# A macaron block on one core: the last chunk of the second feed-forward part in split fp16, and the row sums of the attention's output at another place

## The reference

```
x = x + 0.5 * ffn(layernorm(x))
x = x + attention(layernorm(x))
x = x + 0.5 * ffn(layernorm(x))

ffn(x):  m = k0 * x[s-1] + k1 * x[s] + k2 * x[s+1]        # mixing of neighbouring rows
         h = m @ W1[p] + b1[p];  y[p] = h @ W2[p] + b2[p]     # 9 paths of width 64
         best = argmax(tanh(m @ Wo1 + bo1) @ Wo2 + bo2)
         return layernorm(x + y[best]) * gamma + beta

attention(x): q, k, v = x @ W.T + b
         weights = softmax(abs(q @ k.T / 16), causal)
         return (weights @ v) @ Wo.T + bo
```

## Time and profile before

| what | value |
|---|---|
| median of 3 runs | 1481.22 us (1480.94 to 1482.33) |
| the profiled execution | 1480.94 us |
| its span, first to last instruction | 1479.2 us |
| mean granted TensorE clock | 0.969 |
| TensorE busy | 1353.5 us (92%) |
| VectorE busy | 1168.7 us (79%) |
| ScalarE busy | 926.0 us (63%) |
| GpSimd busy | 315.9 us (21%) |

### The profile page before, as it was taken

The page is one execution under the profiler, slowest core; times in us unless marked ns, Lnnn a source line. Parts: engine busy times, 40 slices in busy tenths (PEclk is TensorE's granted clock), DMA queues, the critical chain, the costliest instruction groups (busy, mean ns, idle before and its releaser), DMA issues.

```text
span 1479.2 us, 25761 instructions
## 1 busy us (share of the span) xinstructions
PE 1353.5 (92%) x7572; PEld 786.7 (53%) x7572; DVE 1168.7 (79%) x2327; ACT 926.0 (63%) x1733; POOL 315.9 (21%) x359
## 2 busy tenths in 40 slices
PE   3999999958999999998968999999998959999995
PEld 2567776734455454544434455454544436777764
DVE  5999998766777777778867777777778857989986
ACT  5666766265666757665755666757665766776641
POOL 2255544440101000000040101000000023555422
PEclk9899999979999999999989999999999969999998
DMA  5143433210010000103010010000103021333221
GB/s 155 50 126 105 119 107 91 88 58 1 29 44 16 28 29 1 44 0 113 2 45 1 29 44 16 28 29 0 44 0 114 1 74 50 105 106 107 91 77 59
DMA packets 86995, 82.26 MB, mean 56 GB/s; under 512 B 8540, under 2 KB 86885, under 8 KB 86885
## 3 DMA queue, kind: packets, MB, share of 16 engines
q1 hardware_dynamic: 86884, 80.91, 18.1%
HBM read 55.43 MB, written 25.46 MB: 55 GB/s over the span
## 4 chain that ended last, share of the span: by engine, by line
PE 74%; DVE 8%; issue 8%; ACT 6%; POOL 2%; DMA 0%; ACTq 0%; DVEq 0%; POOLq 0%; SPq 0%
PE PS L1411 63%; PE PS L1606 3%; PE PS L1419 2%; PE PS L1507 2%; PE PS L1480 1%; DVE R L973 1%; ACT R L1261 1%; POOL R L578 1%; ACT R L1298 1%; ACT R L1302 1%; DVE st L711 1%; PE PS L1489 1%; DVE R L967 1%; DVE R L795 1%; POOL y_rstd L568 1%
## 5 line engine op out<-in xcount | busy, mean ns | idle before, releaser
L1411 PE MATMUL PS<-R 128*128 128x512 f16 (+3 forms) x3456 | 715.1, 362 | 29.3 <-DVE R L973 20.3
L1411 PEld LDWEIGHTS PS<-R 128*128 128x128 f16 (+1 forms) x3456 | 327.5, 98 | 394.1 <-DVE R L973 35.3
L973 DVE TENSOR_TENSOR R<-R 128x512 f16<-128x512 f32 (+3 forms) x288 | 188.7, 655 | 97.4 <-ACT R L1302 96.0
L1289 ACT ACTIVATE R<-PS 128x512 f32 (+5 forms) x288 | 160.2, 558 | 164.9 <-PE PS L1411 164.4
L1298 ACT ACTIVATE R<-R 128x512 f32 (+4 forms) x288 | 169.6, 589 | 51.4 <-DVE R L967 49.9
L1411 PE MATMUL PS<-R,w_hi 128*128 128x512 f16 x640 | 196.9, 390 | 4.3 <-DVE R L780 4.3
L967 DVE TENSOR_TENSOR R<-R,max_row 128x512 f32 (+4 forms) x288 | 187.2, 650 | 7.7 <-ACT max_row L1335 7.7
L1411 PE MATMUL PS<-w_hi,R 128*128 128x256 f16 x1024 | 187.7, 273 | 4.8 <-DVE R L786 4.8
L1302 ACT ACTIVATE R<-R 128x512 f16<-128x512 f32 (+3 forms) x288 | 171.1, 594 | 26.4
L545 POOL TENSOR_SCALAR veps<-mv 128x4 f32<-128x4 f32 x48 | 13.5, 280 | 801.2 <-DVE mv L718 658.1
L961 DVE TENSOR_TENSOR run_max<-run_max,R 128x512 f32<-128x512 f32 (+3 forms) x272 | 174.0, 640 | 9.3 <-DVE run_max L961 1.7
(11 more groups left out here) (116 smaller groups left out, 1710.4 us busy)
## 6 DMA issues: line engine op xcount, KB each, us to landing
R<-x_scratch SPq DMA_DIRECT2D x48, 512.0 KB, 4.5
x_scratch<-R SPq DMA_DIRECT2D x32, 512.0 KB, 3.1
R<-oh_scratch SPq DMA_DIRECT2D x32, 320.0 KB
R<-in_L_attn_x SPq DMA_DIRECT2D x16, 512.0 KB, 5.4
R<-oh_scratch SPq DMA_DIRECT2D x32, 256.0 KB
out<-R SPq DMA_DIRECT2D x16, 512.0 KB, 3.1
R<-in_L_ffn_W SPq DMA_DIRECT2D x2, 288.0 KB
R<-in_L_ffn_W SPq DMA_DIRECT2D x1, 512.0 KB
```

Source lines behind the costliest of these rows:

```text
L973: v.tensor_tensor(p_lo[:, i * TT + lo:(i + 1) * TT], pf[:, (i % 2) * TT + lo:(i % 2 + 1) * TT], p_hi[:, i * TT + lo:(i + 1) * TT], ALU.sub ...
L1289: a.activation(cols(ring, ring_m + i * TT + lo, TT - lo), ps_s[:, i, lo:], ACT.Abs, scale=1.0 / (QS * XS * D ** 0.5)).then_inc(abs_done, 1)
L1411: ins = t_.matmul(dst, w, xx, start=start and n == 0, stop=stop and n == last, skip_group_check=skip)
```

## The change

`whole` is now true in `ffn(0)` only. In `ffn(1)` chunk 4 is split like the others: ScalarE has `masked_high` for a third group, VectorE `masked_low` for a third group (behind that of the second), and TensorE three fp16 products per row group where it had one in fp32. `groups_before` counts three groups per tile there. In the attention, `output` on VectorE now calls `output_sums` itself: behind the output of row group u the sums of u - 1, and behind the last both that are left. The blocks of sums in `first_pair` are gone. At the end of a batch the order is what it was.

```
-            return c == LAST
+            return ph == 0 and c == LAST
...
-            return use(ph, t) * (len(GROUPS) - 1)
+            return t * (len(GROUPS) - 1) if ph == 0 else NTT * (len(GROUPS) - 1) + t * len(GROUPS)
...
                                            scalar=rden[:, u:u + 1], in1=cols(rows, u * D, D),
                                            op0=ALU.mult, op1=ALU.add).then_inc(x2_done, 1)
+                    if u >= 1:
+                        output_sums(s, u - 1, rows)
+                    if u == SUB - 1:
+                        output_sums(s, u, rows)
+
                 def output_sums(s, u, rows):
                     dve.wait_ge(x2_done, SUB * s + u + 1)
                     v.bn_stats(sums_at(s, u), cols(rows, u * D, D)).then_inc(x2_sums, 1)
...
                     def first_pair(i):
-                        if i == 0:
-                            for u in range(SUB):
-                                output_sums(s - 2, u, xr)
                         if is_int(j, NT - 1):
                             for u in ((), (0, 1), (2,), (3,), ())[i]:
                                 output(s - 1, u, xr_beside)
-                            if i == SUB:
-                                for u in range(SUB):
-                                    output_sums(s - 1, u, xr_beside)
...
                 for u in range(SUB):
                     output(b * NT + NT - 1, u)
-                    if u >= 1:
-                        output_sums(b * NT + NT - 1, u - 1, xr)
-                output_sums(b * NT + NT - 1, SUB - 1, xr)
                 first_stats(b + 1, range(1, EARLY))
```

## The result

| | median | runs |
|---|---|---|
| before | 1482.46 us | 6 (1480.94 to 1484.83) |
| after | 1491.96 us | 6 (1491.01 to 1493.11) |
| ratio | 1.0064 | 95% interval 1.0052 to 1.0078 |

The change costs 9.5 us where 3.9 were predicted. The sign is right, the size is not. (The forecast of 1485.1 us stood on before's median of 1481.22 in three runs; with six it is 1482.46, and that is 1.2 of the 6.9 us between forecast and measurement.) The profiled execution of after took 1492.41 us, its span is 1490.6 us and its mean granted clock 0.972. That is 11.4 us more span than before, but the profiled execution of before was the fastest of its six: the first attention step began at 333.19 there, and between 332.93 and 336.08 in the thirteen profiles of this study, whatever the kernel. So I compare by stages.

A forecast was written before the change was run, and what follows sets the result against it. Steady parts were taken as bound by TensorE, with a TensorE-VectorE loop in the second feed-forward part close behind. Terms +0.1 + 4.1 - 0.3 = +3.9 us on a median of 1481.22 gave 1485.1 us, range 1481.0 to 1487.6.

The forecast's parts named there:

- The loop and the turn: Second feed-forward part: TensorE and VectorE wait on each other in turn; the subtraction lengthens this from 14.82 to 15.42 us.
- path start: TensorE's path product of the next tile's chunk 0, held until VectorE's result frees two PSUM banks; at least 1.27 us later.
- Turn by turn: Second feed-forward part: gains of 0.41, 1.17 and 0.41 us, then losses of 0.45 and 0.60 per turn; sum +0.1 us.
- ScalarE's conversion at nothing: Second feed-forward part: one more conversion per tile fits 2.76 us of ScalarE idle time; uncovered, up to 0.6 us per turn.
- Part A: Second feed-forward part: last chunk in three fp16 products, with one more conversion and subtraction per tile; +0.1 us.
- Part B, steps 2 to 4: Attention: two moved row sums delay the maximum, so TensorE waits 0.68 us, in 3 steps x 2 batches; +4.1 us.
- Steps 5 and 6: Attention: no key statistics there, so 0.66 us of moved sums fits VectorE's 1.39 us wait for the transposes; no cost.
- Part B, step 7: Attention: with the sums moved, the maximum comes 0.5 us later but VectorE has two sums fewer; -0.15 us per batch.
- 2: Attention: TensorE's wait in steps 2 to 4 is made good inside the step; whole -0.2 us, 1481.0 us; chance 0.10.
- 4: Second feed-forward part: GpSimd and VectorE lock each other, +3.5 us more, 1488.6 us; chance 0.08.
- 3: Attention step 7 gains in full, 1.31 us per batch, -2.6 instead of -0.3 us: 1482.8 us; chance 0.12.
- rival 1: Second feed-forward part: subtraction hidden, turns of 15.14 us; 1478.8 us (chance 0.08), or 1474.7 with Part B's cost hidden (0.02).

The follow-up runs named there:

- a_late: Kernel before with Part A alone, conversion behind the next turn's scores, subtraction behind the next masking of chunk 2, all tiles: 1485.39 us, ratio 1.0021.
- a_early: Kernel before with Part A alone, conversion behind the next turn's scores, subtraction ahead of the masking of chunk 0: 1478.58 us, ratio 0.9970.
- a_tile0: Kernel before with Part A alone, the first tile's new conversion and subtraction one turn later: 1482.32 us, ratio 0.9998.
- a_only: Kernel before with Part A alone, conversion and subtraction where the change puts them: 1486.29 us, ratio 1.0027.

## Right and wrong, point by point

- **The loop and the turn (right).** 15.42 us were predicted, 15.44 measured, with the 0.28 us of waiting at the path start, and `a_late` and `a_early` show that the subtraction's place sets it. From the result of tile 14 to the end of the span it is 20.1 us before and after, also as said.
- **Turn by turn (sum right, places partly wrong).** From the result of tile 0 to that of tile 14 the prediction's terms sum to +0.5 us (its 0.1 less the first turn's -0.41). The traces give 0.62 - 0.67 + 0.60 = +0.55. But turn 1 lost 0.62 instead of gaining 0.13: the result of tile 0 still waited for TensorE, and so did the way from it (7.74 us to the masking of chunk 3, from 1255.97 to 1263.71), and behind that VectorE's longer part counted in full (8.43 us to the result at 1272.14; 7.80 before). Turn 11 lost nothing, where 0.45 was put: the 14.68 us that the prediction read (1413.28 to 1427.96) are turn 12's alone, and turn 11 took 15.19 before. Turn 13 took 14.77 before and lost 0.15, where 0.60 was put. Behind the wait for tile 13's result, half clock added 1.4 to 1.7 us in four profiles of five, which no term had.
- **ScalarE's conversion at nothing (wrong, the step that failed).** The prediction put this term at nothing, and at 0.6 us per turn if the cover went. The cover (2.76 us of idle time before the transposes) was read in a steady turn and used for all. In the fill turn there are no path products on TensorE, so the transposes come early and the cover is absent (the steady turn is the earlier trace rows). The first turn's -0.41 did come, since chunk 4's products take 1.31 instead of 1.72 us of TensorE; the conversion took it back and more: 1.68 us of wait, and 1.66 of half clock behind it in three profiles of four. By the timed runs it is 3.4 to 4.0 us where it was moved away, and 2.2 where it was added alone. With the half clock of turn 14, each weighted by how often the profiles show it, Part A comes to 0.1 + 1.68 + 0.75 x 1.66 + 0.8 x 1.6 = 4.3 us, against +3.7 measured. By the same sum `a_tile0` should stand at +1.4 and was measured at -0.3 (-1.6 to +1.0), so the share of half clock in turn 14 is probably less than these few profiles say.
- **Part B, steps 2 to 4 (right).** 0.68 x 6 = 4.1 us predicted; the starts of the maximum fall back by 0.64 each (in step 1 they are 351.43 before and 354.32 after, in step 2 382.87 and 386.40, in step 3 425.52 and 429.70), 3.8 in all. Steps 5 and 6: nothing, as said.
- **Part B, step 7 (right in sum).** The maximum came 0.48 later, and behind the first pair the shift was down to 4.59 us from 5.28 (the lower half at 697.57 before, 702.16 after). Net -0.2 us per batch; -0.15 was predicted.
- **Rivals.** 2 and 4 didn't happen, 3 neither; rival 1 is what `a_early` made true by an edit. The prediction had no rival in which the fill of a stage pays, and its range ended 4.4 us short. Of the 6.9 us between forecast and measurement, 1.2 are before's median, 3.6 are Part A, and the other 2 are what the two parts cost only together, which stays open.

## What to carry to other kernels

Idle time that hides an added operation has to be read in the first and last turns of a pipeline too, not only in a steady one: there the neighbours that made the idle time are missing. Ask which instruction stands behind the added one on its engine, and for which engine that one works. And before moving an operation with both inputs in SBUF into an idle gap on VectorE, look at what GpSimd does in that gap.

## What the runs showed of the hardware

- A wait of TensorE can cost more than its length. Behind waits of 2.45 and 2.59 us products ran at half clock (the level of 1.2 GHz instead of 2.4) for about 3 us in seven of nine cases, and at full clock in two (`a_only` in the fill, after in turn 14). It also followed a wait of 1.98 us in `a_late` (turn 14), but none of the waits of 1.56 to 1.98 us at the same place in the seven other profiles. Each time it cost 1.4 to 1.7 us. I did not find what decides it.
- A subtraction of VectorE that began 1.07 us into GpSimd's addition was held for the rest of it (`a_late`), while two maskings out of PSUM beside the same addition (1333.44) took 1.40 us, 0.70 each.
- The time between the two batches, with TensorE at half clock for a part of it, differs by 4.5 us between seven executions of the same attention code (93.07 to 97.55 us).
- Like VectorE in `a_late`, GpSimd seems to be held too. Its operation of 128x4 at line 554 takes 0.23 us in the attention (384.70 in before). In the turns it takes 2.29 us before (1305.02) and 2.89 after, 0.60 more, the length of the new subtraction. It starts inside VectorE's two subtractions (1346.44) and ends at 1349.49, 0.09 us behind VectorE's addition (1348.18 + 1.22). That it is held by these VectorE operations is read from the times alone; no run tests it. The row of after:

```profile
1346.60 2.89 POOL L554 TENSOR_SCALAR neg<-mv 128x4 f32<-128x4 f32 x1
```
